# Attention in a layer stack: two normalisations and the key halves moved by two units of the hand-written order

## The reference, cut to what matters

```python
def _layernorm(x, axis=-1, eps=1e-05): ...          # (x - mean) / sqrt(var + eps)
qkv = _layernorm(x) @ W_attn + b_attn
q, k, v = jnp.split(qkv, 3, axis=2)                 # 16 heads; q and k rotated
att = jnp.einsum('bhqd,bhkd->bhqk', q, k) / sqrt(16)
att = softmax(where(causal, att, -inf))
y = einsum('bhqk,bhkd->bhqd', att, v) @ W_proj + b_proj
x1 = x + _layernorm(y)                              # and xn1 = _layernorm(x1) for the next block
```

## Time and profile before

| what | value |
|---|---|
| time of 3 runs | 3515.46, 3524.84, 3532.96 us; median 3524.84 |
| the profiled execution's own time, and its span | 3520.16 us, 3518.2 us |
| PE, DVE, ACT, POOL busy over the span | 82%, 54%, 36%, 20% |
| mean granted TensorE clock | 0.909 of full speed |
| attention of 8 batches | until about 1500 us; one steady batch takes 181 us |

### The profile page before, as it was taken

How to read it: one execution, slowest core, us unless ns; L and a number is a source line. 1 busy time by engine, 2 the same in 40 slices (tenths; PEclk the granted TensorE clock), 3 DMA queues, 4 the chain that set the end, 5 groups by cost and what they waited for, 6 DMA issues and landing times. The chain is left out here.

```text
span 3518.2 us, 44483 instructions
## 1 busy us (share of the span) xinstructions
PE 2899.9 (82%) x15561; PEld 1776.5 (50%) x15561; DVE 1912.7 (54%) x5455; ACT 1262.4 (36%) x2117; POOL 714.6 (20%) x1101
## 2 busy tenths in 40 slices
PE   3899898989898989823788886579898989989876
PEld 1344343434343434322677765455665656566554
DVE  2766666657575757564566565444525344353442
ACT  1465555555555555621222220113132131322311
POOL 5031414140404040110112112011302112020211
PEclk8799999999999999966988897789999999999998
DMA  4241414141424232131322222200101001010000
GB/s 127 59 128 44 151 44 151 44 151 44 137 58 121 74 109 74 38 118 43 104 72 97 84 96 72 79 18 22 51 0 51 21 30 51 0 51 12 12 24 12
DMA packets 172169, 235.41 MB, mean 67 GB/s; under 512 B 17117, under 2 KB 138873, under 8 KB 165762
## 3 DMA queue, kind: packets, MB, share of 16 engines
q1 hardware_dynamic: 172002, 233.27, 21.6%
HBM read 131.74 MB, written 101.50 MB: 66 GB/s over the span
## 5 line engine op out<-in xcount | busy, mean ns | idle before, releaser
L942 ACT ACTIVATE pt<-ps 128x1024 f32<-128x1024 f32 (+3 forms) x768 | 601.0, 811 | 336.0 <-PE ps L857 225.0
L769 DVE CUSTOM_DVE_ANT_0 masked<-ps,mask_q 128x128 bf16<-128x128 f32 (+3 forms) x1024 | 473.8, 484 | 279.3 <-PE ps L835 275.5
L835 PE MATMUL ps<-sk,sq 96*128 96x512 bf16 (+3 forms) x1536 | 442.1, 346 | 80.6 <-DMA sk<-scratch_stacks 27.6
L854 PE MATMUL ps<-sq,sk 99*128 99x512 bf16 (+3 forms) x1536 | 416.6, 339 | 63.8 <-DMA sq<-scratch_nm_parts 33.2
L773 DVE TENSOR_REDUCE mx<-ps 128x1 f32<-128x512 f32 x512 | 351.8, 687 | 156.8 <-PE ps L835 156.3
L835 PEld LDWEIGHTS ps<-sk,sq 96*128 96x128 bf16 x1536 | 136.9, 99 | 411.5 <-issue 125.6
L873 PE MATMUL ps<-pt,val 128*32 128x512 f32 (+3 forms) x3072 | 334.3, 508 | 1.1 <-ACT yt L950 0.9
L854 PEld LDWEIGHTS ps<-sq,sk 99*128 99x128 bf16 x1536 | 152.6, 101 | 209.3 <-ACT pt L942 76.5
L1948 PE MATMUL ps<-eht,w_fc 128*128 128x512 f32 x512 | 249.7, 636 | 9.5 <-ACT eht L1999 9.5
L1960 PE MATMUL ps<-w_fc,eyb 128*128 128x256 f32 x1024 | 228.7, 381 | 15.5 <-ACT eyb L2007 15.5
L1960 PEld LDWEIGHTS ps<-w_fc,eyb 128*128 128x128 f32 x1024 | 193.3, 190 | 53.7 <-ACT eyb L2007 24.5
(11 more groups left out here) (294 smaller groups left out, 4866.8 us busy)
## 6 DMA issues: line engine op xcount, KB each, us to landing
scratch_stacks<-part SPq DMA_DIRECT2D x32, 768.0 KB, 3.6
sq<-scratch_stacks SPq DMA_DIRECT2D x32, 768.0 KB, 7.9
sk<-scratch_stacks SPq DMA_DIRECT2D x32, 768.0 KB, 9.1
scratch_stacks<-part SPq DMA_DIRECT2D x32, 512.0 KB, 4.5
x<-in_L_attn_x SPq DMA_DIRECT2D x8, 1024.0 KB, 14.3
scratch_stacks<-part SPq DMA_DIRECT2D x32, 256.0 KB, 4.9
xr<-in_L_attn_x SPq DMA_DIRECT2D x8, 1024.0 KB, 6.1
scratch_x<-xr SPq DMA_DIRECT2D x8, 1024.0 KB, 10.3
```

The lines of the kernel that those rows point to most:

```text
L769: nc.vector.tensor_tensor_reduce(mem["masked"][:, slot, 0:n], ps[:, RING[slot], 0:n], mem["mask_q"][:, BANK - n:BANK], 1.0, -3e38, ALU.add ...
L835: nc.tensor.matmul(ps[:, bank, 0:n], sq[0:ROWS, h, i * P:(i + 1) * P], sk[0:ROWS, h, half * BANK:half * BANK + n], start=True, stop=True)\
L854: last = nc.tensor.matmul(ps[:, bank, 0:n], sk[0:ROWS_M, h, j * P:(j + 1) * P], sq[0:ROWS_M, h, q0:q0 + n], start=True, stop=not diag)
L942: nc.scalar.activation(pt[:, u % 3, 2 * pair:2 * pair + 2, 0:n], ps[:, bank:bank + 2, 0:n], ACT.Exp, scale=SCALE).then_inc(e["exp_done"], 1)
```

## The change

It moves steps by whole units and alters no instruction. `x_norm` goes from units 9 to 12 to units 11 to 14, and `xt` one unit later, to 14 and 15. The k halves of `parts` go from 20 and 21 to 22 and 23 (chunk 0) and from 28 and 29 to 30 and 31 (chunk 1); those of q stay. `a_norm` goes from 19 to 22 to 21 to 24 and `x1_stat` from 22 to 25 to 24 to 27.

```diff
             for t in range(4):
                 put(before + 5 + t, *[("x_stat", b, j) for j in tiles[2 * t:2 * t + 2]])
-                put(before + 9 + t, *[("x_norm", b, j) for j in tiles[2 * t:2 * t + 2]])
-            put(before + 13, ("xt", b, 0, 0), ("xt", b, 0, 1))
-            put(before + 14, ("xt", b, 1, 0), ("xt", b, 1, 1))
+                put(before + 11 + t, *[("x_norm", b, j) for j in tiles[2 * t:2 * t + 2]])
+            put(before + 14, ("xt", b, 0, 0), ("xt", b, 0, 1))
+            put(before + 15, ("xt", b, 1, 0), ("xt", b, 1, 1))
             for chunk in range(KC):
                 at = before + 16 + 8 * chunk
...
-                put(at + 4, ("parts", b, 1, chunk, 0))
-                put(at + 5, ("parts", b, 1, chunk, 1))
+                put(at + 6, ("parts", b, 1, chunk, 0))
+                put(at + 7, ("parts", b, 1, chunk, 1))
...
         for t in range(4):
-            put(behind + 19 + t, *[("a_norm", b, j) for j in tiles[2 * t:2 * t + 2]])
-            put(behind + 22 + t, *[("x1_stat", b, j) for j in tiles[2 * t:2 * t + 2]])
+            put(behind + 21 + t, *[("a_norm", b, j) for j in tiles[2 * t:2 * t + 2]])
+            put(behind + 24 + t, *[("x1_stat", b, j) for j in tiles[2 * t:2 * t + 2]])
```

## The result

| | before | changed |
|---|---|---|
| median | 3523.03 us (4 runs, 3515.46 to 3532.96) | 3439.70 us (4 runs, 3430.88 to 3443.38) |
| ratio, 95% interval | | 0.9754 (0.9728 to 0.9779) |
| profiled span | 3518.2 us | 3440.7 us |
| granted clock over the span | 0.909 | 0.920 |

The forecast was 3442 us. A second set of runs of the changed kernel gave 3436.86 us against 3526.21, ratio 0.9737 (0.9716 to 0.9757).

A forecast was written before the change was run, and what follows sets the result against it. PE was taken as the bound (163.6 of 181 us a batch), with idleness and low clock to gain: 38.4 + 48.6 - 2 - 2 = 83 us off 3520.2 gives 3437, as median 3442 us; own range 3427 to 3455, 8 in 10 3427 to 3480.

The forecast's parts named there:

- Stall A: Unit 10: PE waits 3.56 us because ACT comes to x_norm before POOL's shift; removal gains 38.4 us with clock.
- the margin: Unit 11: ACT would reach x_norm 0 to 2 us after POOL has the shift.
- The maxima of unit 9: Needed by unit 12's first scores; expected there with 3 us of margin, so no new wait for their transfer.
- Stall B: Unit 24: PE waits 5.0 us for maxima that POOL takes up late; gain 48.6 us, clock included, in six batches.
- stall C: Unit 34: ACT waits for the statistics behind x1_stat, 3.5 us for PE; counted unchanged.
- the 3 us set aside: Unit 24: low clock behind the short wait left there, half of about 1 us in six batches.
- What the k halves do: Unit 21: POOL had a k half and two residual sums before the maxima; moved with a_norm, maxima taken up at once.
- Moved work: Friction: 2 us for xt one unit later, 2 us for a_norm and x1_stat pairs moved into units 23 to 27.
- The other queues: POOL, ACT and SP work behind the moved steps was to cost nothing; second k half 5.5 us early for ACT.
- Rival 5: Slower: second k half of chunk 0 late for ACT's qk copy, so PE waits; 3543 us or more, chance 0.03.
- The clock's price: Work at half clock takes twice as long: 1.7 us more behind unit 10's wait, 3.2 behind unit 24's.
- The rule on transfers: Unit 24: two 24 KB transfers take 4.1 us by the skill, 3.6 by trace; maxima 0.5 us later, sum 3 smaller.

The follow-up runs named there:

- experiment 1: Only x_norm (two units later) and xt (one unit later) moved, against the kernel before: 3481.5 us, ratio 0.9878.
- edit 1: The part of the change that moves only x_norm and xt; alone against the kernel before: 3481.5 us, ratio 0.9878.
- experiment 3: Only a_norm and x1_stat moved two units later, against the kernel before: 3478.4 us, ratio 0.9886.
- experiment 2: Only the k halves moved two units later, against the kernel before: 3493.9 us, ratio 0.9919.
- experiments 8 and 9: 8: changed kernel with xn1 and score two units later as well, 3415.4 us; 9: the same with score four units later still, 3406.4 us.
- experiment 7: Kernel before with 20 filling matmuls in front of the unit 24 wait in batches 1 to 6: 3501.7 us, ratio 0.9923.
- experiment 4: Changed kernel without the move of the k halves: 3442.4 us, ratio 0.9780 against the kernel before.

## Why the prediction was right, point by point

- *Stall A.* ACT's wait went, as forecast, by the shift's time alone; the margin was 1.0 us, forecast 0 to 2. The maxima of unit 9 did not become the next wait (experiment 1). The term was sized at 36 us net and measured 38 by the launch and 46 by the stretch. Its own share is as forecast: PE's idle time fell by 21 us (forecast 22), and the low clock behind the seven stalls had cost 14 us. The other 10 to 11 us are low clock behind waits that the edit left as they were. Summed over the 10 us behind each, it cost 5.1 us less behind the six stalls B, 4.5 less behind the six stalls C and 1.7 less behind the first wait of batch 7. It depends on when the wait falls, which no row of the kernel before could tell, and the prediction has no term for it.
- *Stall B.* The landing of the maxima, 0.5 us late by forecast, was 0.43 to 0.66 us late in five batches of six. Counted from ACT's copy, unit 24 starts 5.1 us sooner in the mean, forecast 5.4. The clock stayed at 1.00 behind these waits, even the 1.43 us one, so the 3 us set aside for it were not needed. The row that they were taken from covers only a part: behind the 1.35 us wait the clock stood at 0.50 from about 1354.5 to 1357.9, and the window of the earlier trace rows begins in the middle of it, so that wait cost 1.7 us of clock and not 1. Forecast 47 us, measured 43.6 by a_norm alone and 41 to 44 by the whole change less edit 1, both by the stretch.
- *What the k halves do.* The prediction took this together with a_norm as one step. The sum was right, but its sentence that POOL "had a k half and two residual sums" in front of the maxima tells only half of the cause. Moving a_norm alone takes most of the stall away with the half where it was (experiment 3), and so does moving the k halves alone (experiment 2). The cause is POOL's idle wait for ACT at the first a_norm sum together with all that is queued behind it; either edit breaks it, so their gains don't add.
- *Moved work.* 4 us of friction were set aside. PE's idle time in the stretch fell by 50 us, and the waits of stalls A and B alone account for 51, so the stretch shows about 1 us. DVE and ACT did have room at 23 to 27. The same move at 36 to 39 did meet a full DVE (experiments 8 and 9).
- *The other queues.* Between units 12 and 33 no wait of PE is over 1 us but the one of 1.43 at unit 24, which is what is left of stall B, and none stands before L881 or L892. Rival 5 needed the second k half to be late; ACT never waited for it.
- *The clock's price.* Half speed counted as half the work lost: shown by experiment 7.
- *The rule on transfers.* By the fixed cost and the rate that the Trainium skill gives ("DMA: Bandwidth & Descriptors", Anatomy of one DMA), the prediction's estimate for the two transfers was 4.1 us. They took 3.6 us in most batches and 4.6 at 688.21, so the rows were the better guide for the usual case.
- *The sum.* The forecast's 83 us are 53 of PE's idle time and 30 of low clock. The stretch shows 50 and 40. So the waits are right within 3 us. The clock gave back 10 us more, nearly all of it seen: the 3 us set aside at stall B, 4 us behind stall C and 2 behind the first wait of batch 7, which the change does not touch. By the launch the gain is 83 us in the first set and 89 in the second, by the stretch 87.5 to 89.8, and in the first profile the part behind attention was 10 us longer, which the change does not explain. The mechanism and its size are shown; that the first set meets the forecast to 1 us is luck.

## What to carry to other kernels

In a hand-written order of in-order engines, look for the instruction that stands waiting with work queued behind it, and not only for the longest instruction in front of the late one: moving the step that POOL waited in by two units let the blocks behind it run first, and took away 4.6 us of a delay of 5.5 us that seemed to belong to a 3.7 us block. Price a wait of PE with the low clock behind it, which was 40% of the cost of stall B here. Look at PE's idle time and its busy time apart before a gain is put down to an edit: some 10 us of experiment 1 were low clock behind other waits. And before moving work into later units, look at the busy time of the engines in those very units, since the same edit gave all it promised at one place and half at another.

## What the runs showed of the hardware that was not expected

- The same wait of 3.5 us (stall C) cost 1.7 us of clock in some batches and 2.9 in others of the changed kernel: the clock over the next 8 us was 0.79 in three batches and 0.64 in three. In the kernel before it was 0.61 to 0.63 in all six.
- Behind a wait of 1.35 us the clock fell to 0.53 in the stretch of the earlier trace rows, behind one of 1.51 us to 0.67 (experiment 2), and behind one of 1.43 us not at all (1.00 from 688.2 to 694.2); behind 2.70 us it fell and behind 2.11 us not (both experiment 4). Which short waits cost clock could not be told from their length.
- 120 additional matmuls, put where PE stood waiting, made the kernel 17 to 24 us faster.
- The 24 KB transfer of the maxima took 1.5 us from its issue to that of the second transfer in most batches, but 2.2 and 2.95 us in single ones.
